# Attention and feed-forward on eight cores: the value matmuls of two tiles in every second slot, side work paced by lengths, and one tile's statistics moved ahead

## What is computed

```
x = L0_attn_x                                   # (4, 4096, 1024), float32
r = layernorm(x)
q = einsum('bnd,hkd->bnhk', r, query_proj)      # 16 heads of 64
k = einsum('bmd,dk->bmk', r, key_proj)          # one key head
v = einsum('bmd,dv->bmv', r, value_proj)        # one value head
attn = softmax(einsum('bnhk,bmk->bnhm', q, k) / 8)
x = x + einsum('bnhv,dhv->bnd', einsum('bnhm,bmv->bnhv', attn, v), output_proj)
s = einsum('btd,dm->btm', layernorm(x), Win) + bin_
h = relu(s[..., None] * W1 + b1)                # 64 channels x 16
g = einsum('btmh,mh->btm', h, W2) + b2
out = x + einsum('btm,md->btd', g, Wout) + bout
```

## Time and profile before

| | us |
|---|---|
| median of 3 runs | 1018.16 |
| the runs | 1018.16, 1017.29, 1019.68 |
| the profiled execution | 1017.6 |
| its span on the slowest core (core 4) | 1016.1 |
| its spans on cores 0 to 7 | 1015.4, 1014.4, 1014.1, 1012.9, 1016.1, 1015.2, 1015.1, 1015.3 |
| first exponential starts, last one starts (core 4) | 24.2, 984.6 |
| ACT busy | 952.2 (94%) |
| PE busy, PE weight loads | 900.6 (89%), 493.1 (49%) |
| DVE busy | 358.7 (35%) |
| POOL busy | 56.5 (6%) |

### The profile page before, as it was taken

How to read it: one execution, slowest core, us unless ns; L and a number is a source line. 1 busy time by engine, 2 the same in 40 slices (tenths; PEclk the granted TensorE clock), 3 DMA queues, 4 the chain that set the end, 5 groups by cost and what they waited for, 6 DMA issues and landing times.

```text
span 1016.1 us, 28595 instructions; the slowest of 8 cores (1012.9 to 1016.1 us)
## 1 busy us (share of the span) xinstructions
PE 900.6 (89%) x11582; PEld 493.1 (49%) x11712; DVE 358.7 (35%) x637; ACT 952.2 (94%) x1043; POOL 56.5 (6%) x131
## 2 busy tenths in 40 slices
PE   3898899998899999998889999998889998898884
PEld 3445555555444545544444454544444554454442
DVE  4535666652512222234202122244202326424215
ACT  2597999999999999999999999999999999999981
POOL 3201111100000000000000000000000000000000
PEclk9999999999999999999999999999999999999995
DMA  8502257220000000002200000001210000400101
GB/s 196 138 12 85 85 119 174 85 85 3 1 2 2 2 2 2 2 2 84 85 2 2 1 3 1 2 2 62 58 51 2 2 2 2 167 2 1 44 2 41
DMA packets 13406, 40.94 MB, mean 40 GB/s; under 512 B 3168, under 2 KB 3296, under 8 KB 13152
## 3 DMA queue, kind: packets, MB, share of 16 engines
q1 hardware_dynamic: 8208, 26.26, 8.5%
q0 software_dynamic: 4784, 12.32, 5.3%
q10 hardware_dynamic: 288, 0.52, 0.1%
HBM read 35.70 MB, written 8.39 MB: 43 GB/s over the span
## 4 chain that ended last, share of the span: by engine, by line
ACT 80%; issue 9%; PE 5%; DVE 3%; DMA 3%; POOL 0%; DVEq 0%; SPq 0%; POOLq 0%; ACTq 0%
ACT ptu L816 80%; DMA xtra<-x_own 2%; PE ob L457 1%; DMA xbuf<-x_own 1%; PE spa L662 1%; PE spb L662 1%; DVE r1u L478 1%; PE sda L380 0%; DVE r1t L504 0%; DVE lnst L468 0%; PE spb L695 0%; DVE lnst L469 0%; DVE gacc L787 0%; POOL rstd L838 0%; PE sdb L391 0%
## 5 line engine op out<-in xcount | busy, mean ns | idle before, releaser
L816 ACT ACTIVATE ptu<-spa 128x1024 bf16<-128x1024 f32 x512 | 594.5, 1161 | 17.7 <-PE spa L662 17.6
L816 ACT ACTIVATE ptu<-spb 128x1024 bf16<-128x1024 f32 x512 | 595.9, 1164 | 2.9 <-PE spb L662 2.9
L457 PE MATMUL ob<-vab,ptu 128*128 128x65 bf16 x8192 | 409.1, 195 | 0.7 <-ACT ptu L816 0.5
L457 PEld LDWEIGHTS ob<-vab,ptu 128*128 128x128 bf16 x8192 | 298.4, 97 | 208.4 <-issue 208.4
L662 PE MATMUL spb<-qt,k2t 64*128 64x512 bf16 x1024 | 200.8, 380 | 40.5 <-ACT ptu L816 34.9
L662 PE MATMUL spa<-qt,k2t 64*128 64x512 bf16 x1024 | 200.9, 380 | 36.5 <-ACT ptu L816 28.3
L662 PEld LDWEIGHTS spb<-qt,k2t 64*128 64x128 bf16 x1024 | 63.4, 92 | 127.2 <-issue 108.1
L662 PEld LDWEIGHTS spa<-qt,k2t 64*128 64x128 bf16 x1024 | 62.6, 92 | 114.5 <-issue 95.1
L725 DVE TENSOR_TENSOR oacc<-oacc,ob 128x520 f32<-128x520 f32 x50 | 34.8, 696 | 77.3 <-PE ob L457 77.2
L836 POOL TENSOR_SCALAR lnve<-lnmv 128x1 f32<-128x1 f32 x48 | 12.7, 264 | 658.0 <-DVE lnmv L471 658.0
L527 DVE TENSOR_TENSOR xbuf<-xbuf,sda 128x512 f32<-128x512 f32 x16 | 11.0, 688 | 93.3 <-PE sda L423 80.0
(11 more groups left out here) (123 smaller groups left out, 471.1 us busy)
## 6 DMA issues: line engine op xcount, KB each, us to landing
xbuf<-x_own SPq DMA_DIRECT2D x28, 512.0 KB, 4.4
xbuf<-x_oth SPq DMA_DIRECT2D x16, 512.0 KB, 3.9
out<-xbuf POOLq DMA_DIRECT2D x14, 512.0 KB, 3.6
wqb<-wq POOLq DMA_DIRECT2D x8, 256.0 KB, 9.6
xtra<-x_own SPq DMA_DIRECT2D x4, 512.0 KB, 6.9
xtra<-wp POOLq DMA_DIRECT2D x1, 2048.0 KB, 21.0
boutbc_s<-boutbc SPq DMA_DIRECT2D x1, 512.0 KB, 12.7
out<-xbuf SPq DMA_DIRECT2D x2, 256.0 KB, 2.6
```

Source lines behind the costliest of these rows:

```text
L457: r = te.matmul(osum[:, hd, c * 65:(c + 1) * 65], ptu[:, g % NPT, hd * 512 + c * 128:hd * 512 + (c + 1) * 128], vab[:, a + i, :], start=(i ...
L816: sc.activation(ptu[:, g % NPT, :], sps[g % 2][:], AF.Exp, scale=0.125).then_inc(ex, 1)
```

## The change

Four things change; the arithmetic does not.

1. `pv_at` gives four halves (16 value matmuls, those of two tiles) in every odd slot of a segment and none in the even ones. In segments of 32 tiles the first ones stand in slots 2 and 3, and from 5 on every second.
2. `pace` counts lengths in hundredths of a microsecond: a slot is 92, scores 22, a switch between scores and other matmuls 20, a half 12, a piece 22. It keeps how far PE lags (`pe_lag`) and adds pieces as long as that stays within `PE_LAG` 45, wherever the slot is; in blocks 1 to 3 only in slots with halves (from the third slot of a segment on). DVE's pieces have lengths of their own and a lag of up to 40. Forced pieces that the halves need (values) now stand behind the slot's scores (`pe_v`), not ahead.
3. A tile's statistics are two pieces of DVE's side work (`ln_stats_a`, `ln_stats_b`) instead of one.
4. At the start DVE does the statistics of the fifth tile (index 4) ahead of the fourth tile's normalization, and SP loads tile i (4 to 7) once tile i-3 has landed instead of i-2.

```diff
-    d = 1 if SEGS[s][0] == 0 else 2
-    if r < d:
-        return []
-    if r < 3 * d:
-        return list(range(3 * (r - d), 3 * (r - d) + 3))
-    return [2 * r, 2 * r + 1]
+    if SEGS[s][0] > 0 and r < 4:
+        return [[], [], [0, 1, 2, 3], [4, 5, 6, 7]][r]
+    return list(range(2 * r - 2, 2 * r + 2)) if r % 2 else []
...
+SLOT = 92
+SCORES = 22
+SWITCH = 20
+HALF = 12
+PIECE = 22
+PE_LAG = 45
+DVE_LAG = 40
...
-        halves = len(pv_at(s, g - SEG_AT[s]))
-        for _ in range({0: 2, 2: 1, 3: 0}[halves]):
-            if head["pe"] is not None and ok(head["pe"], 1):
-                run("pe", pe, "pe1")
-
-        if g + 1 != SEG_AT[s + 1] and head["dve"] is not None and ok(head["dve"], 1):
-            run("dve", dve, "dve1")
+        halves = pv_at(s, g - SEG_AT[s])
+        forced += force([("sev", USE_NO["V", (SEGS[s][2] + h // 2) // 4, 0] + 1) for h in halves], "_v")
+
+        pe_lag = min(pe_lag + PIECE * forced, PE_LAG)
+        t = SCORES + HALF * len(halves) + (SWITCH if halves or forced else 0)
+        switch = 0 if halves or forced else SWITCH
+        while head["pe"] is not None and ok(head["pe"], 1):
+            if not halves and SEGS[s][0] > 0 and g - SEG_AT[s] > 1:
+                break
+            if pe_lag + t + switch + PIECE - SLOT > PE_LAG:
+                break
+            run("pe", pe, "pe")
+            t += switch + PIECE
+            switch = 0
+        pe_lag = max(0, pe_lag + t - SLOT)
+
+        room = SLOT + (0 if g + 1 in SEG_AT else DVE_LAG)
+        while head["dve"] is not None and ok(head["dve"][0], 1) and dve_lag + head["dve"][1] <= room:
+            dve_lag += head["dve"][1]
+            run("dve", dve, "dve")
+        dve_lag = max(0, dve_lag - SLOT)
...
+        def ln_stats_a(v, li):
             q = li % 4
             wait_x(v, li)
             v.bn_stats(lnst[:, q, 0:6], xt(li)[:, 0:512])
+
+        def ln_stats_b(v, li):
+            q = li % 4
             v.bn_stats(lnst[:, q, 6:12], xt(li)[:, 512:1024]).then_inc(bns, 1)
             v.wait_ge(bns, li + 1)
             v.bn_aggr(lnmv[:, q, :], lnst[:, q, :]).then_inc(agg, 1)
...
             for g in range(-2, NG):
-                run(gen, counts["pe0"].get(g, 0))
+                run(gen, counts["pe_s"].get(g, 0))
...
+                run(gen, counts["pe_v"].get(g, 0))
                 if g >= 0:
...
-                run(gen, counts["pe1"].get(g, 0))
+                run(gen, counts["pe"].get(g, 0))
...
             ln_stats(v, 3)
+            ln_stats(v, 4)
             ln_norm(v, 3)
...
             for i in range(4, 8):
-                wait_x(e, i - 2)
+                wait_x(e, i - 3)
                 e.dma_start(xt(i), xtile(i)).then_inc(xtl[i - 4], 16)
```

More of the change, by code:

```diff
@@ L151, in pace @@
     head = {"pe": next(pe), "dve": next(dve)}
-    counts = {"pe0": {}, "pe1": {}, "dve0": {}, "dve1": {}}
+    counts = {w: {} for w in ("pe_s", "pe_v", "pe", "dve_s", "dve_v", "dve")}
     def run(which, gen, where):
@@ L156, in run, with force @@
         head[which] = next(gen, None)
-    credit = 0
+    def force(want, where):
+        n = 0
+        while not ok(want, 0):
+            if head["pe"] is not None and ok(head["pe"], 0):
+                run("pe", pe, "pe" + where)
+                n += 1
+            else:
+                assert head["dve"] is not None and ok(head["dve"][0], 0), (now, head)
+                run("dve", dve, "dve" + where)
+        return n
+    pe_lag = dve_lag = 0
     for g in range(-2, NG + 1):
         now[0] = g
-        want = []
+        forced = 0
         if g + 2 < NG:
-            k, hp, a, b = SEGS[SEG_OF[g + 2]]
-            mc = a + g + 2 - SEG_AT[SEG_OF[g + 2]]
-            want += [("sev", USE_NO.get(q, -1) + 1) for q in queries_of(SEG_OF[g + 2])]
+            s = SEG_OF[g + 2]
+            mc = SEGS[s][2] + g + 2 - SEG_AT[s]
+            want = [("sev", USE_NO.get(q, -1) + 1) for q in queries_of(s)]
             want.append(("sev", USE_NO.get(("K", mc // 4, 0), -1) + 1))
-        if 0 <= g < NG:
-            s = SEG_OF[g]
-            for h in pv_at(s, g - SEG_AT[s]):
-                want.append(("sev", USE_NO["V", (SEGS[s][2] + h // 2) // 4, 0] + 1))
-        for s in range(len(SEGS)):
-            if last_part(s) and g == SEG_AT[s + 1]:
-                note("onr", 8 * SEGS[s][0] + SEGS[s][1] + 1)
-        while not ok(want, 0):
-            if head["pe"] is not None and ok(head["pe"], 0):
-                run("pe", pe, "pe0")
-            else:
-                assert head["dve"] is not None and ok(head["dve"], 0), (g, head)
-                run("dve", dve, "dve0")
+            forced += force(want, "_s")
+        ends = [s for s in range(len(SEGS)) if g == SEG_AT[s + 1]]
+        for s in ends:
+            if last_part(s):
+                note("onr", 8 * SEGS[s][0] + SEGS[s][1] + 1)
+            dve_lag += 110 if last_part(s) else 75
         if g < 0 or g >= NG:
@@ L471, in ln_stats @@
             v.bn_aggr(lnmv[:, q, :], lnst[:, q, :]).then_inc(agg, 1)
+        def ln_stats(v, li):
+            ln_stats_a(v, li)
+            ln_stats_b(v, li)
         def ln_norm(v, li):
@@ L481, in dve_side @@
         def dve_side(v, note):
-            stats = norms = 4
+            stats, norms = 5, 4
+            note("agg", stats)
             late = []
@@ L489, in dve_side @@
                     while ahead and stats <= ahead[-1]:
-                        yield []
-                        ln_stats(v, stats)
+                        yield [], 70
+                        ln_stats_a(v, stats)
+                        yield [], 90
+                        ln_stats_b(v, stats)
                         stats += 1
@@ L500, in dve_side @@
                 bank = side[n % 2]
-                yield [("smd", n + 1)]
+                yield [("smd", n + 1)], 42 if kind in ("V", "ot") else 70
                 v.wait_ge(smd, n + 1)
@@ L554, in dve_side @@
                     li = NTILES + a
-                    yield []
+                    yield [], 70
                     v.wait_ge(sev, n + 1)
-                    ln_stats(v, li)
+                    ln_stats_a(v, li)
+                    yield [], 90
+                    ln_stats_b(v, li)
                     note("agg", li + 1)
@@ L759, in _ @@
             for g in range(-2, NG + 1):
-                run(gen, counts["dve0"].get(g, 0))
+                run(gen, counts["dve_s"].get(g, 0))
                 if g > 0 and g in SEG_AT:
@@ L765, in _ @@
                     v.scalar_tensor_tensor(b1adj[:], w1p[:], bin2[:], b1p[:], op0=ALU.mult, op1=ALU.add)
-                run(gen, counts["dve1"].get(g, 0))
+                run(gen, counts["dve_v"].get(g, 0))
+                run(gen, counts["dve"].get(g, 0))
             run(gen, 1 << 20)
```

13 lines of the change are left out of this document (6 added, 7 removed).

## The result

| | before | after |
|---|---|---|
| median of the runs, us | 1018.56 (4 runs) | 1056.82 (4 runs, 1055.95 to 1059.73) |
| ratio, 95% interval | | 1.038 [1.036, 1.041] |
| the profiled execution, us | 1017.6 | 1059.7 |
| spans of the cores, us | 1012.9 to 1016.1 | 1052.4, 1053.1, 1049.6, 1053.9, 1058.2, 1049.3, 1053.8, 1048.9 |

The account below looks back on a forecast made before the run. ACT was taken as the bound. From 1017.6 us, gains of 0.4, 2.2, 3.0, 0.9 and 1.1 and a loss of 0.3 give 1010.3; late scores add 33.2, 1.1 and 4.8: 1049.4, predicted 1049 us, range 1028 to 1060.

Parts of the forecast that it names:

- ACT is the bound, scores may be 0.32 us late: Scores may start 0.32 us after the end of the exponential that frees their tile; every later 0.01 us is lost.
- The full slot is 1.36 us, the next scores 0.59 late, 0.27 lost: Blocks 1 to 3: sixteen value matmuls and two pieces take 1.36 us, making the next scores 0.27 us too late.
- Every second pair, 123 losses, 33.2 + 1.1 us: Blocks 1 to 3: 123 losses of 0.27 make 33.2 us; one-piece slots and block starts with transposed pieces add 1.1.
- the small ones: Small waits of ACT such as at exponentials 854 and 949, 3.3 us in all; a third, 1.1 us, may go.
- Block 0: 4.8 us, 3 to 7: Late scores in block 0, from lone full slots and slots with three or four pieces, lose 4.8 us together.
- Start: 0.4 us gained: First exponential 0.1 to 0.2 us later, scores of 4 about 31.0 instead of 31.43; gain 0.4 us, bounds 0 to 1.5.
- Exponential 16, 64 and 67: 2.2, 3.0 and 0.9 us: Gains at three waits of ACT: 2.2 us at 16, net 3.0 at 64 (2.66 still lost there), 0.9 at 67.
- End: 0.3: Behind the last exponential stand sixteen value matmuls instead of eight: 0.26 us later, value 0.3.
- the lag is hidden: Rival: scores 0.59 us after the freeing end are in time, only the gains stay; 1010 us, chance 12%.
- the burst is shorter: Rival: 0.2 us of switches hide under the longer burst, each loss is 0.07; 1024 us, chance 7%.
- every pair loses: Rival: ACT doesn't stay behind for the next pair, 231 losses by 0.27 make 62 us; 1078 us, chance 2%.
- the clock falls between pairs: Rival: pairs without pieces leave PE idle 0.7 us; ten clock falls of 1.33 us cost 13 us; 1062 us, chance 3%.

Follow-up runs that it names:

- experiment 1: The changed kernel with side pieces of blocks 1 to 3 only in slots without value matmuls; 1032.1 us, ratio 1.014.
- experiment 2: The changed kernel with at most one side piece in each slot from the third slot of a segment of blocks 1 to 3; 1032.6 us, ratio 1.014.
- experiment 9: The changed kernel with the 2048 KB load of output weights cut into eight transfers, one behind each of tiles 20 to 27; 1053.55 us, ratio 1.033.
- experiment 12: The kernel before with the loads of win, wout and wp issued behind tile 19 instead of tile 20; 1021.4 us, ratio 1.003.
- experiment 4: The kernel before with the changed start alone: fifth tile's statistics ahead of the fourth's normalization, loads of tiles 4 to 7 earlier; 1018.4 us, ratio 1.000.
- experiment 8: As experiment 7, but where side work is forced the planner takes a piece of DVE before a piece of PE; 1021.4 us, ratio 1.003.
- experiment 3: The kernel before with the new `pv_at`, the old planner, and two pieces only in slots without halves; 1020.8 us, ratio 1.004.
- experiment 11: Experiment 7 with the load of output weights (wp) split into eight transfers; 1015.5 us, ratio 0.996 against the kernel before.
- experiment 7: The changed kernel with value matmuls back in the places of the kernel before and `PE_LAG` 17 instead of 45; 1018.2 us, ratio 1.000.

## Why the prediction was right, and where it was off

It said 1049 us, 1028 to 1060, slower; 1056.8 was measured.

- *ACT is the bound, scores may be 0.32 us late.* Right: 0.58 late lost 0.26, 0.32 late lost nothing, and in experiments 1 and 2 lateness of 0.36 to 0.48 lost 0.05 to 0.16. In block 0 of experiment 9, core 7, 0.52 late lost 0.20 and 0.70 late lost 0.38: the lateness less 0.32 each time.
- *The full slot is 1.36 us, the next scores 0.59 late, 0.27 lost.* Measured 1.35, 0.58 and 0.26.
- *Every second pair, 123 losses, 33.2 + 1.1 us.* Right: 127 losses over 0.2 us behind exponential 256 in blocks 1 to 3 (all cores alike), 114 of them by 0.26 (29.7 us), the other 13 by 0.33 to 0.70 (6.3 us). The blocks lost 35.0 us more than before. What the sum missed is that seven of the 13 fall on an exponential at which ACT loses 0.1 us anyway (every 64th) and then cost 0.53 to 0.55. The 1.1 us hoped for from the small ones did not show as a gain: those at 854 and 949 are gone, new ones at 454, 486 and 936 (0.4 each) took their place.
- *Block 0: 4.8 us, 3 to 7.* Without the stop (experiment 9) it is 4.1 more than before, and the places are those of the forecast: seven losses of 0.26 to 0.28 us (exponentials 68, 74, 98, 126, 134, 150 and 178) behind the seven lone slots of sixteen value matmuls and two pieces, and 0.20 behind four key pieces in a slot (109, 161, 183). With it, cores 2, 5 and 7, whose stop was short, lost 4.9 us more than before, the others up to 8.4. Here the step failed that looked only at PE and DVE for lateness. The order showed DVE's statistics moved ahead, but I didn't follow that to the transfer that POOL issues behind tile 20. Experiments 9 and 12 show what it costs.
- *Start: 0.4 us gained.* Nothing: 8 lost 6.50 instead of 6.68 where the clock held, 1 to 7 the same 3.5. On three cores (one in the kernel before) a low clock came in at 8 and took 1.5 us; core 4's late load and the low clock behind it took 3.5 us and made it the slowest core by 4.3 us, which a forecast from mean cores can't have. Experiment 4 measured the start as 1.000 of before; the low clock at 8 came on four of its cores, and whether the new start brings it stays open.
- *Exponential 16, 64 and 67: 2.2, 3.0 and 0.9 us.* 9 to 61 gained 1.6 (16 itself 1.9, new small ones took the rest), 62 to 67 3.5. The loss at 64 was forecast as 2.66 and is 2.67. But its working was right by luck: the 32 value matmuls that it counted lie beside the copy of the keys, as experiment 8 shows, and the copy, which it left out, is about as long.
- *End: 0.3.* 0.4.
- *The rivals.* That the lag is hidden, that the burst is shorter and that every pair loses are all excluded by the rows above. That the clock falls between pairs is excluded by the 1.00 of the stretch, and from 159 to 1019 us the clock is 1.00 on all cores; it fell behind the stops, for which the rival gave no place.

Mean over the cores, the span grew by 37.6 us, forecast were 31.8: 1.8 of the difference are in blocks 1 to 3 with the small ones, 1.7 in block 0 (the stops 2.4, the rest 0.7 less than forecast), 1.1 the start, 1.0 exponentials 9 to 67. The slowest core adds the rest.

What stays open: when a packet of instructions is asked for, and so how long it waits (core 0 shows none for 14 us beside the 2048 KB, while packets of other queues move); what moved tile 20 ahead in experiment 3; and where the rest of experiment 11's gain on experiment 7 comes from.

## What to carry to other kernels

When an engine is the bound and another feeds it through two buffers, the planner's bound on the feeder's lag must be what the buffers forgive, read from an isolated late case of the trace (here 0.32 us of lateness, 0.15 of it used already), and a lag is only paid back by the air of the following slots, 0.02 us each where they are nearly full. Paced by length, the same matmuls in the same pairs lose 37, 13 or 2.4 us in blocks 1 to 3: with pieces behind the value matmuls, with pieces in the other slots, and there with a bound of 14 instead of 45. And when work on one engine moves earlier, follow what other queues do on its signal: a large transfer issued 8 us earlier cost up to 4.2 us on a core (9.4 against 5.2), and in eight parts, spread over 40 us, next to nothing.
